# A scan-plus-mixer layer in 16 chunks: the last chunks closed by halves, r from scaled weights, small scalars moved to ScalarE, and a new order of work

## What is computed

```python
h  = layernorm(x)                                   # LN1
x1, z = split(h @ W_in)                             # 256 + 256 columns
proj = x1 @ W_x                                     # delta_raw (256), B (16), C (16)
delta = softplus(proj[:256] @ W_dt + b_dt)
for n in 16 states:  s_n = exp(-delta*exp(A_log_n)) * s_n + (delta*x1)*B_n     # scan over time
y  = (sum_n s_n * C_n + x1*D_param) * silu(z) @ W_out
x  = x + layernorm(y + h) * ln_g + ln_b             # LN2
h  = layernorm(x)                                   # LN3
xr = mu_r*h + (1-mu_r)*h_prev ; xk = mu_k*h + (1-mu_k)*h_prev    # h_prev: the token before
x  = x + sigmoid(xr @ W_r.T) * (relu(xk @ W_k.T)**2 @ W_v.T)
```

## Time and profile before

| | us |
|---|---|
| median of the runs | 1037.73 |
| profiled execution, its own time | 1038.93 |
| its span (first to last instruction) | 1037.2 |
| PE / DVE / ACT / POOL busy | 905.7 / 925.7 / 907.3 / 939.1 |
| granted TensorE clock, mean | 0.934 of full |

### The profile page before, as it was taken

How to read it: one execution, slowest core, us unless ns; L and a number is a source line. 1 busy time by engine, 2 the same in 40 slices (tenths; PEclk the granted TensorE clock), 3 DMA queues, 4 the chain that set the end, 5 groups by cost and what they waited for, 6 DMA issues and landing times. The chain is left out here.

```text
span 1037.2 us, 15069 instructions
## 1 busy us (share of the span) xinstructions
PE 905.7 (87%) x4728; PEld 699.3 (67%) x4728; DVE 925.7 (89%) x1003; ACT 907.3 (87%) x2041; POOL 939.1 (91%) x455
## 2 busy tenths in 40 slices
PE   6485888989898998989899898989989898996976
PEld 3254576867767686776768577676858677684954
DVE  0799899999999999999999999999999999999933
ACT  5886889999989999999989999999999999886753
POOL 0799999999999999999999999999999999999810
PEclk9797898999899998999999998999989998998998
DMA  4534454444535544463455545354554445254111
GB/s 141 218 123 185 166 203 182 163 166 179 189 135 212 187 184 158 170 223 125 183 186 183 195 150 206 129 203 161 187 219 151 178 166 207 100 206 180 62 41 41
DMA packets 51039, 172.21 MB, mean 166 GB/s; under 512 B 5392, under 2 KB 31760, under 8 KB 34576
## 3 DMA queue, kind: packets, MB, share of 16 engines
q1 hardware_dynamic: 50960, 171.25, 45.0%
HBM read 153.41 MB, written 9.44 MB: 157 GB/s over the span
## 5 line engine op out<-in xcount | busy, mean ns | idle before, releaser
L450 POOL TENSOR_TENSOR dbx<-u,b_ring 128x1024 f32<-128x1024 f32 x256 | 602.5, 2371 | 0.7 <-DVE u L850 0.7
L545 ACT ACTIVATE da_ps<-delta,a_neg 128x512 f32<-128x512 f32 x512 | 334.7, 682 | 38.8 <-DVE hg L802 14.1
L463 POOL TENSOR_TENSOR hg<-hg,c_ring 128x1024 f32<-128x1024 f32 x144 | 341.9, 2374 | 3.8 <-DVE hg L802 3.8
L952 PEld LDWEIGHTS y_ps<-ident,hg 128*128 128x128 f32 x2048 | 252.0, 149 | 74.0 <-issue 48.3
L952 PE MATMUL y_ps<-ident,hg 128*128 128x128 f32 x2048 | 277.1, 286 | 15.4 <-POOL hg L463 14.6
L802 DVE TENSOR_TENSOR_SCAN hg<-da_ps,carry,dbx 128x512 f32<-128x512 f32 x216 | 264.1, 1267 | 12.8 <-ACT da_ps L545 12.5
L802 DVE TENSOR_TENSOR_SCAN da_ps<-da_ps,carry,dbx 128x512 f32<-128x512 f32 x168 | 206.1, 1272 | 1.1 <-ACT da_ps L545 1.1
L809 DVE TENSOR_TENSOR hg<-da_ps,c_ring 128x1024 f32<-128x1024 f32 x112 | 137.2, 1225 | 12.0 <-DVE da_ps L802 0.5
L802 DVE TENSOR_TENSOR_SCAN hg<-da_ps,dbx 128x512 f32<-128x512 f32 x72 | 84.5, 1207 | 7.9 <-ACT da_ps L545 7.6
L972 PE MATMUL w_ps<-ident,h_tok 128*128 128x128 f32 x128 | 26.9, 350 | 60.9 <-DVE mixed L859 60.8
L959 PE MATMUL w_ps<-mixed,w_kT 128*128 128x512 f32 x128 | 64.9, 632 | 6.8 <-DVE mixed L859 3.7
(11 more groups left out here) (134 smaller groups left out, 1468.5 us busy)
## 6 DMA issues: line engine op xcount, KB each, us to landing
b_ring<-bc_rows_dram SPq DMA_DIRECT2D x64, 1024.0 KB, 5.3
c_ring<-bc_rows_dram SPq DMA_DIRECT2D x64, 1024.0 KB, 4.7
x_tok<-in_L_attn_x_in_dram SPq DMA_DIRECT2D x16, 512.0 KB, 5.8
res<-xn_tok SPq DMA_DIRECT2D x16, 512.0 KB, 3.2
xres<-in_L_attn_x_in_dram SPq DMA_DIRECT2D x16, 512.0 KB, 4.7
out_dram<-r_out SPq DMA_DIRECT2D x15, 512.0 KB, 3.0
bc_rows_dram<-bc_rows SPq DMA_DIRECT2D x16, 64.0 KB, 1.6
w_in<-in_L_attn_W_in_dram SPq DMA_DIRECT2D x1, 512.0 KB, 4.8
```

The source lines that it names most:

```text
L450: pool.tensor_tensor(dbx[:, n % X_RING, :, :], u[:, ip, :, :], b.to_broadcast([P, KH, LC]), ALU.mult).then_inc(s["dbx_done"], 1)
L463: pool.tensor_tensor(part, part, c_of(n).to_broadcast([P, KH, LC]), ALU.mult).then_inc(s["g_pool"], 1)
L545: act.activation(da_of(n, h), delta[:, ip, h, :], ACT.Exp, scale=a_neg[:, h, n:n + 1]).then_inc(s["da_ready"], 1)
L952: last = pe.matmul(y_tok[:, b, h * P:(h + 1) * P], hg[:, n % H_RING, h, b * P:(b + 1) * P], ident[:, :], is_transpose=True, start=n == 0 a ...
```

## The change

Four parts, in one diff.

1. **r by scaled weights.** ScalarE writes h unscaled into h_of instead of (1-mu_r)*h; DVE's mix keeps only the mu_k half. Instead of one W_r there are two weights, W_r scaled by mu_r and by (1-mu_r), made once at the start, and PE applies both, the second to the tokens shifted by one.
2. **Small scalars on ScalarE.** nr = nm*rs of LN1 and LN3 become four 128x1 activations each, nm3 one 128x4 activation. POOL keeps only its products.
3. **The end.** END of chunk 14 (marked `late_`) is done inside step 15; chunk 15 is closed by a new `close()` in two halves of 256 tokens, each with its own PSUM regions and semaphores. The last column's product is shared, half 0 on POOL, half 1 on DVE; mu_r for chunk 15 is again by mixing, with W_r loaded and turned again; LN3's mean and variance come from bn_stats on DVE.
4. **Order.** All the tables are new, Y_LAG goes from 1 to 2, and in step -1 `turn_ffn_weights` and `center_w_out` stand earlier.

```diff
-B_LEAD, C_LAG, Y_LAG = 3, 1, 1
+B_LEAD, C_LAG, Y_LAG = 3, 1, 2
-POOL_TURN = dict(nm3=11, nr3=13, nr1=15)
-VEC_TURN = dict(mix1=1, mix0=2, gate=3, sp0=8, u0=9, sp1=11, x20=11, x21=11, u1=12, v0=13, v1=13)
+VEC_TURN = dict(mix0=3, mix1=3, gate=4, sp0=5, u0=6, x21=10, x20=11, sp1=12, u1=13, v0=13, v1=14)
...
+            def r_by_token(out, v):
+                for b in range(2):
+                    at_b = (2 * v + b) * P
+                    for k in range(KH):
+                        pe.matmul(by_block(out)[:, b, :], h_of[:, k, at_b + 1:at_b + 1 + P], w_rT[:, k, :], start=k == 0,
+                                  stop=False)
+                    for k in range(KH):
+                        last = pe.matmul(by_block(out)[:, b, :], h_of[:, k, at_b:at_b + P], w_r_prev[:, k, :], start=False,
+                                         stop=k == KH - 1)
...
                     act.activation(xk[:, m, 1:LC + 1], b[:, :], ACT.Copy, scale=omk[:, m:m + 1])
-                    act.activation(xr[:, m, 1:LC + 1], b[:, :], ACT.Copy,
-                                   scale=omr[:, m:m + 1]).then_inc(mixed_prev[m], 1)
+                    act.activation(h_of[:, m, 1:LC + 1], b[:, :], ACT.Copy).then_inc(mixed_prev[m], 1)
...
+                if ln in nr:
+                    need(act, ln_rs[ln], count)
+                    for j in range(TB):
+                        last = act.activation(nr[ln][:, j:j + 1], nm[ln][:, j:j + 1], ACT.Copy, scale=rs[ln][:, j:j + 1])
+                    last.then_inc(ln_nr[ln], 1)
...
-                        act.sem_inc(ln_sum[3], 1)
+                        act.activation(nm[3][:, :], sum3[:, :], ACT.Copy, scale=-1.0 / D).then_inc(ln_sum[3], 1)
...
-            step(NT - 1, 1, scan=True, mid=True, end=True)
-            step(NT, 0, mid=True, end=True)
-            step(NT + 1, 1, end=True)
+            step(NT - 1, 1, scan=True, mid=True, end=True, late=True)
+            close()
...
+                dve.wait_ge(last_y, 1)
+                gate(0)
+                dve.wait_ge(s["y_added"], NS * NT)
+                gate(1)
+                second(0)
+                mean_of(0)
+                second(1)
+                norm(0)
```

More of the change, by code:

```diff
@@ L223, in mamba_rwkv_layer @@
         ln_nr = {ln: sem(f"ln{ln}_nr") for ln in nm}
+        last_y = sem("last_y")
+        (last_gated, last_turned, last_kept, last_wo, last_sq, last_lv2, last_rs2, last_g, last_x2, last_bn, last_mean,
+         last_lv3, last_rs3, last_norm, last_hT, last_share, last_mix, last_k, last_r, last_relu, last_kact, last_tanh,
+         last_v, last_gv, last_out) = [
+            [sem(f"last_{name}{v}") for v in range(2)]
+            for name in """gated turned kept wo sq lv2 rs2 g x2 bn mean lv3 rs3 norm hT share mix k r relu kact tanh v gv
+            out""".split()]
         work_ready = [sem(f"work_ready{b}") for b in range(W_BANKS)]
@@ L408, in step @@
                     load_c(t, 3)
-                if scan:
+                if scan and not late:
                     if mid:
@@ L552, in keep_carries, with step @@
                                ACT.Copy).then_inc(s["carry_saved"], k)
-            def step(t, par, pre=False, scan=False, mid=False, end=False, more=False):
+            def step(t, par, pre=False, scan=False, mid=False, end=False, late=False, more=False):
                 nxt = 1 - par
@@ L756, in _ @@
+            steps(act, step, close)
         @block.vector
@@ L884, in step @@
                         small_constants()
-                    for m in range(2):
-                        if end and at(f"mix{m}"):
-                            mix(m)
+                    for mark, c in ended(t, end, late):
+                        for m in range(2):
+                            if at(f"{mark}mix{m}"):
+                                mix(m, mark, c)
                     if mid and at("gate"):
@@ L912, in _ @@
+            steps(dve, step, close)
         @block.tensor
@@ L1095 @@
+            steps(pe, step, close)
 _INS = ["L0_attn_x_in", "L0_attn_W_in", "L0_attn_W_x", "L0_attn_W_dt", "L0_attn_b_dt", "L0_attn_A_log",
```

524 lines of the change are left out of this document (360 added, 164 removed).

## The result

| | before | changed |
|---|---|---|
| median of the runs, us | 1038.22 (4 runs, 1037.49 to 1039.17) | 1013.89 (4 runs, 1011.54 to 1014.61) |
| ratio, 95% interval | | 0.9761 (0.9742 to 0.9780) |
| profiled execution: own time, span | 1038.93, 1037.2 | 1014.46, 1012.7 |

A forecast was written before the change was run, and what follows sets the result against it. The middle was taken as paced by a ring through PE, the mixes and ScalarE's copies, all four lists within 5 us; +2.2 - 0.6 + 0 - 2 + 3.1 - 14.7 = -12.0 gave 1026 us, range 1011 to 1038.

The forecast's parts named there:

- Its own list is therefore 59.8 - 2.4 = 57.4 us a step: Middle steps before the change: ScalarE's own work taken as the 59.8 us step less 2.4 of waits.
- Sum: 57.4 + 1.6 + 0.5 - 0.2 + 0.2 = 59.5: Middle steps: ScalarE's new list, adding nr activations, LN waits with nm3, and ln handovers, less two copy scales; 58.7 to 60.3.
- The price of the new activations: ScalarE in the steady steps: 0.20 us for each small nr activation, eight 1.6 us; bounds 0.10 and 0.30 each.
- So ScalarE's own list becomes the longest, 1.5 us over POOL's, and the step cannot be shorter than it: Middle steps: ScalarE's 59.5 us against POOL's 58.0; the step stays at 59.8, gain 0 over twelve steps.
- Rival 1: Middle steps: small activations cost 0.10 each without waits, steps of 58.8 to 59.2 us, 1016 us in all; chance 0.24.
- The signs: Right: nr starts 0.2 apart, GpSimd waiting 1 to 2 us, ScalarE busy 58 or more; wrong: steps 59 or less.
- Its wait "goes": TensorE in the steady steps: its wait for VectorE's mix, 44.1 us in ten steps, disappears because the banks are apart.
- a gain only if DVE is what others wait for: VectorE in the steady steps: two mixes go, 1.3 us by starts, its list falling to about 56 us.
- its three small operations: GpSimd in the middle steps: 0.15 us each; they and their waits go, leaving a list of 58.0 us.
- Head: Start of the first product: +2.2 us, bounds 1.5 and 4, as x waits for six weight copies on ScalarE.
- Last step: Step 15: column 15's end comes 3.1 us later with END of chunk 14 inside; bounds 0 and +8.
- Close: From the last scan's end to the span's end: 35 us instead of 49.7, gain 14.7; bounds 10 and 18.

The follow-up runs named there:

- e_old_small: Kernel before with only nm3 and nr of both norms moved to ScalarE: 1062.64 us, ratio 1.0228.
- e_nr_twice: Changed kernel with the eight small nr activations issued twice a step on ScalarE: 1031.42 us, ratio 0.9929.
- e_moves: Changed kernel with head and middle steps in the order, banks and lag of the kernel before: 1096.48 us, ratio 1.0562.
- e_bank: Kernel before with hT0 in PSUM bank 1 instead of 2, apart from hT1: 1068.55 us, ratio 1.0292.
- e_small_pool: Changed kernel with nm3 and nr of LN1 and LN3 on GpSimd again, norm3 one turn later: 1065.60 us, ratio 1.0260.
- e_end_only: Kernel before with only the new last step and close: 1038.58 us, ratio 1.0002.
- e_end_act: Kernel before with the new end, and in its last step nm3 and nr of LN3 on ScalarE: 1033.45 us, ratio 0.9948.
- e_head2: Changed kernel with the three weights turned later in the head, between the two additions that make u: 1012.84 us, ratio 0.9753.
- e_nr_vec: Changed kernel with nr of both norms as one 128x4 multiplication each on VectorE: 1124.03 us, ratio 1.0819.
- e_nr1_vec: Changed kernel with nr of LN1 alone as one 128x4 multiplication on VectorE: 1021.11 us, ratio 0.9832.
- e_order: Changed kernel with r mixed by VectorE and small scalars on GpSimd as before: 1065.98 us, ratio 1.0263.

## Why the prediction was wrong, step by step

The time lay in the range, but the gain was twice the forecast, and the forecast's account of the middle was wrong.

- **The step that failed** is "Its own list is therefore 59.8 - 2.4 = 57.4 us a step", and with it "Sum: 57.4 + 1.6 + 0.5 - 0.2 + 0.2 = 59.5". The 57.4 was not work: 54.5 are, and 2.9 are handovers, which belong to the order as much as the named waits do. I let the named waits fall with the new order and carried the handovers over, and added 0.6 of new ones (the waits for rs, for the last nr and for nm3, and the 0.1 twice). Split like the measured step, the forecast was 54.5 + 1.5 = 56.0 of bare list, 3.5 of handovers and 0.3 of named waits; measured are 55.9, 1.7 and 0.9. The mis-sized term is thus the handovers, 1.8 us a step too many, with the named waits 0.6 too few. So the step came out at 58.5 and not 59.8, and twelve times the 1.22 by which the steps fell is the 14.6. e_old_small shows that the same sum comes within 0.7 where the order stays, e_nr_twice that it holds on top of the right base. Why this order has fewer late operands than the old one, unit by unit, stays open.
- **The price of the new activations** was right: 0.20 forecast, 0.19 to 0.20 measured from start to start, the bare list up by 1.4.
- **"So ScalarE's own list becomes the longest, 1.5 us over POOL's, and the step cannot be shorter than it"**: 57.6 is under GpSimd's 58.05. Rival 1 had the place (nothing pulls on GpSimd any more, steps of 58.8 to 59.2) for a wrong reason, cheap activations, and 0.4 to 0.8 us too long. That its 1016 lies nearest to the measured time is luck.
- **The signs.** Of those named for "right", the small activations 0.2 apart, the wait for the mix gone and the clock near 1.0 came, and the last output 31 us after the last scan. GpSimd's wait of 1 to 2 us a step is 0.4, and ScalarE's busy time of 58 us or more is 57.0. Of those for "wrong", steps of 59 us or less came.
- **TensorE**: its clock came back (1.00) and eight more matmuls went in at nothing, as forecast. Its wait "goes": in e_moves, with the old order and banks, it is still 47.4 us in ten steps. Whether the separate banks alone would have done it isn't known, since in e_bank the other bank was shared too.
- **VectorE**: "a gain only if DVE is what others wait for". It is, by 0.5 us a step in the new order.
- **GpSimd**: I priced its three small operations at 0.45 us and their waits at 1.3. What they do to the others is larger: with them on GpSimd the new order is 3.6 us a step longer (e_small_pool), and the last step of e_end_only 3.9 us longer than e_end_act's. I had looked at them as a load only. Of the waits that I put down to ScalarE's sums, the profile names VectorE's u for 3.0 of the 12.9 us.
- **Head** +2.9 for +2.2, within the bounds. Its mechanism (x waits for four scaled and two plain copies) is shown by e_head2.
- **Last step** +5.8 for +3.1, within the bounds of 0 and +8; VectorE waited 0.7 and 1.0 us for v of chunk 14, and 3.9 for y at its gate, which the working did not have.
- **Close** -16.3 for -14.7. The shares and mixes came at about 20 us after the last scan as worked out; k's two halves took 4.8 us where I had 5.2, r 3.5 as forecast, v 3.6 for 3.5; the last output ended 30.8 us after the last scan for 31.4, and the one more unit at the slow clock did not come.
- **A rule of the Trainium skill.** nr on ScalarE cost 1.5 us of bare list a step (80 activations in ten steps, 0.19 each). The Trainium skill (ScalarE: Activation LUTs, Rules for kernel authors) would rather have it on VectorE. e_nr_vec and e_nr1_vec did that, and neither was faster than the changed kernel. By its length alone VectorE would be the better place, 0.15 us for 128x4 against four times 0.19. What spoiled it was that the same multiplication took 5.1 to 6.6 us a step (e_nr_vec) and once 7.92 (e_nr1_vec) where GpSimd's products ran beside it.

## What to carry to other kernels

When an engine's list is taken as step minus named waits, it still holds the short handovers; before such a list is carried over to a new order, work it out from start-to-start distances and keep the handovers apart, since they go with the order. A tiny operation is priced by its place: what is ahead of it and behind it in its queue, and what another engine does at that moment. Nr of LN1 on VectorE took 0.15 us right behind u and 6 us two turns earlier, beside GpSimd's products; so read the length of a moved operation again in the new trace before the queue is blamed. And in the twelve full steps the new order without the moved operations lost 31 us (e_order), the moved operations without it 56 (e_moves), and both together gained 15, so the parts of such a change can't be judged one at a time.
